# A four-layer attention kernel: the row factors of the softmax on ScalarE, a new order of value sums and casts, and the last four steps turned by TensorE

## What is computed

```python
x = _rmsnorm(hidden_states, ln_weight)             # hidden_states: layer-normed rows
h_q = (x @ w_q.T).reshape(b, lq, H, DH)            # H = 32, DH = 128
h_k = (key_value_states @ w_k.T).reshape(b, lk, H, DH)
h_v = (key_value_states @ w_v.T).reshape(b, lk, H, DH)
score = jnp.einsum('bqhd,bkhd->bhqk', h_q, h_k)
score = score + position_bias[None]
score = jnp.where(m, score, -jnp.inf)
score = jax.nn.softmax(score, axis=-1)
score = jnp.where(m, score, 0.0)
attn = jnp.einsum('bhqk,bkhd->bqhd', score, h_v).reshape(b, lq, H * DH)
out = attn @ w_out.T
return hidden_states + out
```

## Time and profile before

| | |
|---|---|
| median of three runs | 1003.94 us (1002.92 to 1004.36) |
| profiled execution | 1005.09 us, its span 1003.1 us |
| mean granted TensorE clock | 0.985 |
| busy: PE, DVE, ACT, POOL | 937.3, 739.3, 598.3, 527.0 us |

### The profile page before, as it was taken

How to read it: one execution, slowest core, us unless ns; L and a number is a source line. 1 busy time by engine, 2 the same in 40 slices (tenths; PEclk the granted TensorE clock), 3 DMA queues, 4 the chain that set the end, 5 groups by cost and what they waited for, 6 DMA issues and landing times.

```text
span 1003.1 us, 17307 instructions
## 1 busy us (share of the span) xinstructions
PE 937.3 (93%) x5261; PEld 796.9 (79%) x5261; DVE 739.3 (74%) x1289; ACT 598.3 (60%) x1847; POOL 527.0 (53%) x582
## 2 busy tenths in 40 slices
PE   9999999999899989998999899989999897889997
PEld 8778888888788878887888778877887776768885
DVE  5676874676787787777787778777877887667787
ACT  5787556465565656665666566656574656344564
POOL 2450636365557656675457555755565643112477
PEclk9999999999999999999999999999999998899999
DMA  9214348644666457645683657364755662130101
GB/s 337 78 65 151 126 153 289 215 167 147 221 223 224 148 213 253 235 146 209 215 269 123 239 184 258 123 248 155 269 166 194 204 216 84 65 116 1 33 22 63
DMA packets 61291, 171.70 MB, mean 171 GB/s; under 512 B 6055, under 2 KB 8491, under 8 KB 60988
## 3 DMA queue, kind: packets, MB, share of 16 engines
q1 hardware_dynamic: 61244, 171.11, 49.6%
HBM read 159.56 MB, written 11.53 MB: 171 GB/s over the span
## 4 chain that ended last, share of the span: by engine, by line
PE 66%; DVE 14%; ACT 8%; issue 8%; POOL 3%; DVEq 1%; DMA 0%; SPq 0%; ACTq 0%; POOLq 0%
PE ps_v L363 5%; PE ps_o L363 5%; PE ps_s L2193 5%; PE ps_o L365 4%; PE ps_o L364 4%; PE ps_v L365 4%; PE ps_v L364 4%; PE ps_q L363 4%; PE ps_q L365 4%; PE ps_q L364 4%; PE ps_k L363 4%; PE ps_k L364 4%; PE ps_k L365 4%; PE ps_t L2214 3%; ACT probs_t L799 3%
## 5 line engine op out<-in xcount | busy, mean ns | idle before, releaser
L799 ACT COPY probs_t<-scores 32x128 f32<-32x128 f32 x768 | 227.6, 296 | 175.8 <-DVE scores L1617 167.6
L787 ACT ACTIVATE scores<-scores,neg_max 128x128 f32<-128x128 f32 x256 | 99.7, 391 | 110.1 <-DVE neg_max L1602 109.7
L1158 POOL TENSOR_TENSOR wq_lo<-raw_q,wq_hi 128x256 fp32r<-128x256 f32 x65 | 57.2, 881 | 150.5 <-ACT wq_hi L620 150.5
L363 PE MATMUL ps_o<-wo_hi,att_hi 128*128 128x512 f32 x256 | 106.4, 416 | 20.0 <-DVE acc L1488 16.2
L1598 DVE TENSOR_TENSOR scores<-ps_s,shift 128x512 f32<-128x512 f32 x64 | 44.2, 691 | 104.4 <-PE ps_s L2193 104.2
L364 PE MATMUL ps_o<-wo_lo,att_hi 128*128 128x512 f32 x256 | 102.4, 400 | 0.0
L365 PE MATMUL ps_o<-wo_hi,att_lo 128*128 128x512 f32 x256 | 102.4, 400 | 0.0
L1488 DVE TENSOR_TENSOR acc<-ps_o,acc 128x512 f32<-128x512 f32 x128 | 86.8, 678 | 17.2 <-PE ps_o L365 17.1
L1476 DVE TENSOR_TENSOR att_lo<-ps_t,att_hi 128x512 fp32r<-128x512 f32 x64 | 44.2, 690 | 65.6 <-ACT att_hi L781 65.6
L1117 POOL TENSOR_TENSOR shift<-bias_sb,mask_sb 128x512 f32<-128x512 f32 x64 | 87.2, 1365 | 1.5 <-DVE scores L1598 1.5
L363 PE MATMUL ps_v<-wv_hi,ct_hi 128*128 128x256 f32 x264 | 78.0, 295 | 6.3 <-DVE vv L1442 2.2
(11 more groups left out here) (394 smaller groups left out, 2850.5 us busy)
## 6 DMA issues: line engine op xcount, KB each, us to landing
ring_hi<-scratch_x_t SPq DMA_DIRECT2D x39, 512.0 KB, 4.0
ring_lo<-scratch_x_t SPq DMA_DIRECT2D x39, 512.0 KB, 4.9
ring_hi<-scratch_c_t SPq DMA_DIRECT2D x39, 512.0 KB, 5.4
ring_lo<-scratch_c_t SPq DMA_DIRECT2D x39, 512.0 KB, 6.2
raw_o<-in_w_o SPq DMA_DIRECT2D x16, 512.0 KB, 3.3
raw_q<-in_w_q SPq DMA_DIRECT2D x15, 512.0 KB, 4.1
raw_k<-in_w_k SPq DMA_DIRECT2D x15, 512.0 KB, 5.2
xt_hi<-scratch_x_t SPq DMA_DIRECT2D x13, 512.0 KB, 5.8
```

The lines of the kernel that those rows point to most:

```text
L363: pe.matmul(dst, hi_l, hi_r, start=first, stop=False)
L787: e = act.activation(probs[n][:, m, :], scores[n][:, m, :], ACT.Exp, bias=neg_max[:, n, m:m + 1], accum_out=row_sum[:, n, m:m + 1])
L799: last = act.copy(block_of(probs_t, j, i), block_of(scores[n], i, j))
L1158: pool.tensor_tensor(w_slot(wq_lo, slot), src, w_slot(wq_hi, slot).bitcast(F32), ALU.subtract).then_inc(wq_lo_s, 1)
```

## The change

1. `scale_rows` is new: for steps 0 to 59 ScalarE multiplies the four tiles by their row factors, with four ACTIVATE Identity instructions whose scale is the column `row_fac`, right behind `attention_high`. VectorE's multiply stays in steps 60 to 63 alone. VectorE makes the row factors (`row_factors`) earlier in its step, and its two transposes wait for ScalarE's signal `scaled`.
2. On VectorE the value sums `v_c22`, `v_u4` (c=0) move ahead of the transposes, others ahead of `add_output` of part 0; in c=3 and c=7 the add of part 0, which stood ahead of the transposes, now stands behind them.
3. On ScalarE the casts of the value weights (`high_v1` to `high_v7` but 4) move ahead of the exponentials, `attention_high` directly behind these; on GpSimd the value weights' low halves come first in their step.
4. On TensorE `output` waits for `att_hi` alone and does the four matmuls that need it first; `att_lo` is waited for ahead of the last two of part 0. In c=1 a unit for k moves ahead of the one for v, in c=4 one for q.
5. In steps 60 to 63 TensorE turns the four tiles (`step_transpose`, into `ps_t`), ScalarE copies them out at once (`pt_evac`), and the values are multiplied within the same step. The order of these steps on TensorE, VectorE and ScalarE is written anew.

No DMA is added, removed or moved.

```diff
+            def scale_rows(s, n):
+                act.wait_ge(s_chain, chain(s, 3))
+                for m in range(4):
+                    e = act.activation(probs[n][:, m, :], probs[n][:, m, :], ACT.Identity, scale=row_fac[:, n, m:m + 1])
+                e.then_inc(scaled, 1)
...
+            def pt_evac(s):
+                act.wait_ge(pt_done, s - WHOLE + 1)
+                act.copy(probs_t[:], blocks(ps_t)).then_inc(pt_out, 1)
...
-            def softmax_back(s, n):
+            def row_factors(s, n):
                 dve.wait_ge(e_done, s + 1)
                 dve.reciprocal(row_inv[:, n, :], row_sum[:, n, :]).then_inc(s_chain, 1)
-                dve.wait_ge(s_chain, 5 * s + 2)
+                dve.wait_ge(s_chain, chain(s, 2))
                 dve.scalar_tensor_tensor(row_fac[:, n, :], row_max[:, n, :], -MASKED / 3.0, row_inv[:, n, :],
                                          ALU.is_gt, ALU.mult).then_inc(s_chain, 1)
-                dve.wait_ge(s_chain, 5 * s + 3)
-                dve.tensor_tensor(probs[n][:], probs[n][:], row_fac[:, n, :].unsqueeze(2).broadcast_to([P, 4, P]),
-                                  ALU.mult).then_inc(s_chain, 1)
 
             def turn_blocks(s, n):
-                dve.wait_ge(s_chain, 5 * s + 4)
+                dve.wait_ge(scaled, s + 2)
                 dve.transpose(flat(probs_t), flat(probs[n])).then_inc(s_chain, 1)
                 dve.transpose(flat(probs[n]), flat(probs[n])).then_inc(p_done, 1)
...
             def output(s, c, g=None, parts=(0, 1)):
 
-                wait_from(pe, att_lo_s, s + 1)
+                wait_from(pe, att_hi_s, s + 1)
...
                     for h in range(2):
-                        last = three(pe, ps_o[:], att_hi[:, 2 * j + h, :], att_lo[:, 2 * j + h, :],
-                                     wo_hi[:, h, :], wo_lo[:, h, :], h == 0, h == 1)
+                        pe.matmul(ps_o[:], att_hi[:, 2 * j + h, :], wo_hi[:, h, :], start=h == 0, stop=False)
+                        pe.matmul(ps_o[:], att_hi[:, 2 * j + h, :], wo_lo[:, h, :], start=False, stop=False)
+                    if j == 0:
+                        wait_from(pe, att_lo_s, s + 1)
+                    for h in range(2):
+                        last = pe.matmul(ps_o[:], att_lo[:, 2 * j + h, :], wo_hi[:, h, :], start=False, stop=h == 1)
...
+            def step_transpose(s, c):
+                pe.wait_ge(p_done, s + 1)
+                wait_from(pe, att_lo_s, s)
+                for m in range(4):
+                    last = pe.transpose(ps_t[:, m * P:(m + 1) * P], probs[c % 2][:, m, :], ident[:])
+                last.then_inc(pt_done, 1)
...
+            g = GROUPS - 1
+            s = STEPS - 4
+            wait_projections(g, 4)
+            step_scores(s, 4)
+            q_p5(g)
+            step_values(s - 1, 3, v_count(TURNS - 1, 13))
+            k_p5(g)
+            v_p4(TURNS - 1, 1)
+            output(s - 1, 3, None, (0,))
+            step_transpose(s, 4)
+            output(s - 1, 3, None, (1,))
+            step_values(s, 4, v_count(TURNS - 1, 14))
```

224 lines of the change are left out of this document (122 added, 102 removed).

## The result

The changed kernel takes 945.49 us in the median of four runs (944.07 to 946.25), the kernel before on the same chip 1003.43 (1001.01 to 1004.36): a ratio of 0.942, with an interval of 0.940 to 0.945. The forecast was 958 with a range of 944 to 984. The profiled execution took 945.47, its span 943.6.

A forecast was written before the change was run, and what follows sets the result against it. TensorE, waiting on VectorE, ScalarE or GpSimd work, was taken as the bound. Gains of 29.4 (turns), 4.5 (clock), 1.0 (small waits) and 11 (last four steps) sum to 45.9 us, giving a median of 958, range 944 to 984.

The forecast's parts named there:

- The turns: Turns 1 to 7: removing TensorE's waits gains 29.4 us, and waits of 0.3 us and less give 1.0.
- (a): Turns: ScalarE's scaling gates VectorE and waits on `acc` stay; median 973.5 us; chance 0.18 with what lies around it.
- The residue: Turns: `acc` waits left over, 0.5 us in c=3 and 0.2 in c=7 of each, 4.9 in all.
- The clock: Turns: the slow clock goes with its stall in c=0, three times at 1.5 us, 4.5 (0 to 5.4).
- The first steps: Steps ahead of turn 1: zero, as ScalarE pays 1.25 us a step and VectorE gives back 0.7 to 1.7.
- (e): Ahead of turn 1: ScalarE's extra 1.25 us in 8 steps costs 10 us unhidden, median 968; chance 0.05.
- The last four steps: Steps 60 to 63: TensorE's transposes and same-step values gain 11 us (bounds 4 and 16).
- The bursts: Last four steps: low-clock matmuls behind the waits go, three or four bursts of about 1.4 us each.
- (c): Last four steps: the clock falls behind the transposes, four bursts of 1.4 us return; median 964; chance 0.09.
- (d): Turns: late q and k low halves make TensorE wait in 56 steps; slower, median 1014 at 1 us; chance 0.05.
- The cover of 5.9 us: c=0: low halves of q and k weights end at 475.87 and are first read at 481.75, 5.9 us later.
- (b): Whole kernel: the change does all it can, 57.2 us gained, median 947; chance 0.10.

The follow-up runs named there:

- experiments 1 and 12: Kernel before with the early value-weight casts and GpSimd's subtractions alone, 1012.57 us; the same with VectorE's negation of the row maxima also gone, 992.27 us.
- experiment 8: Changed kernel with turn 1's c=3 cast, c=4's cast and subtraction, and step 0's value copy mended, and the first eight steps' multiply on VectorE: 940.68 us.
- experiment 2: Kernel before with the value sums of c=0 alone moved ahead of VectorE's multiply and transposes: 991.95 us.
- experiments 4 to 6: Changed kernel with one part undone each: last four steps as before, 960.91 us; output behind `att_lo` again, 950.33; casts and GpSimd's order as before, 968.11.
- experiment 9: Changed kernel with turn 1's c=3 cast, c=4's cast and subtraction, and step 0's value copy mended, the first eight steps' multiply staying on ScalarE: 938.27 us.
- experiment 7: Changed kernel with three more ScalarE copies that compute nothing behind the scaling in each step ahead of the last four: 959.49 us.

## Why the prediction was right in direction and 12 us short

**The turns: 29.4 and 1.0 counted, some 39 measured.** The mechanism holds. The wait for `wv_lo` in c=6 and for `vv` in c=0 are gone, and the scaling takes what was estimated. (a) fell: in turns 2 to 6 VectorE stands before its transposes for the scaling ten times, 4.8 us in all and 0.5 at most, and in c=3 not at all. The failing term is the price of a wait. The listed waits of TensorE in turns 1 to 7 fell from 37.9 to 10.7 us, by 27.2, which is less than the 30.4 of the sum; the turns became some 39 us shorter. The sum took 1.74, 1.55 and 1.2 us as the profile prints idle time, but a wait costs more than the idle time that it shows. TensorE in c=0 of turn 5 in the kernel before, at the same place as the earlier trace rows but at a full clock:

```profile
579.24 0.39 PE L365 MATMUL ps_o<-wo_hi,att_lo 128*128 128x512 f32 x1
581.36 0.39 PE L363 MATMUL ps_v<-wv_hi,ring_hi 128*128 128x256 f32 x1 [1.73 <-DVE vv L1561]
581.58 0.28 PE L364 MATMUL ps_v<-wv_lo,ring_hi 128*128 128x256 f32 x1
581.69 0.28 PE L365 MATMUL ps_v<-wv_hi,ring_lo 128*128 128x256 f32 x1
```

Matmuls overlap: those of 512 columns start every 0.23 us and those of 256 every 0.12, though one takes 0.39 or 0.28. Without the wait the matmul at 581.36 would have started at 579.47, which is 1.89 us sooner and not 1.73; and the one after it starts 0.22 behind it and not 0.12. So the wait costs 1.99, and c=0 did become 2.00 shorter. In c=6 1.55 of idle became 1.81, in this kernel and in experiments 1 and 12. Read in this way, the six listed waits of turn 5 in the kernel before have 5.7 us of idle time and cost 7.3, and the two that are left in after have 0.7 and cost 1.3. That makes 6.0 of the 6.6 us that the turn became shorter; the rest lies in delays of 0.4 us and less that the table of waits doesn't list. In c=7, where the forecast had a wait of 0.6 for `acc`, 1.42 was gained: by the starts `acc` cost 0.85, `kt` behind it 0.49, and an unlisted delay at `att_lo` 0.37, and 0.3 is left.

**The residue: 4.9 counted, 4.8 measured, but elsewhere.** The sum left `acc` 0.5 us in c=3 and 0.2 in c=7 of each turn. In turns 2 to 6 neither stands in the table of waits any more: the add of part 0 in c=3 is in time, since ScalarE had scaled before VectorE came to the transposes. What is left is 0.24 in c=1 of turns 2 to 7, 1.74 in c=3 of turn 1, and 1.63 in c=3 of turn 7, where it was 1.62. That the sums agree is luck. Besides, there are two waits that the prediction didn't see.

First, c=4 is half a microsecond longer in each turn: the negation and GpSimd's subtraction, moved to the front, meet. VectorE, GpSimd and TensorE of after:

```profile
400.92 1.09 DVE L1623 TENSOR_SCALAR neg_max<-row_max 128x4 f32<-128x4 f32 x1
401.93 0.68 DVE L1583 TENSOR_TENSOR v_odd_low<-ps_v,v_odd_low 128x512 f32<-128x512 f32 x1
...
400.70 1.29 POOL L1226 TENSOR_TENSOR wv_lo<-raw_v_even,wv_hi 128x512 fp32r<-128x512 f32 x1 [3.68 <-ACT wv_hi L682]
...
402.66 0.39 PE L372 MATMUL ps_v<-wv_hi,ct_hi 128*128 128x256 f32 x1 [0.49 <-DVE v_odd_low L1583]
```

The prediction asked for each edit what is queued behind it on its own engine. It didn't ask what a GpSimd instruction at a new time does to VectorE, although it had read that pattern itself (1.74 against 0.69 for the multiply).

Second, turn 1 gained 3.3 us and not the 6.6 of turn 5. In c=0, where turn 5 gained 2.0, turn 1 had no wait to lose; but c=3 is 0.7 longer, where in turn 5 it is 1.45 shorter. Its cast of c=3 stands ahead of the exponentials and reads a weight that is free only when the last plain value product has run. ScalarE, then TensorE:

```profile
196.67 0.62 ACT L682 CAST wv_hi<-raw_v_even 128x512 fp32r<-128x512 f32 x1 [9.34 <-PE ps_v L374]
197.20 0.40 ACT L796 ACTIVATE scores<-scores,neg_max 128x128 f32<-128x128 f32 x1
...
199.36 0.50 PE L2206 MATMUL ps_o<-wo_hi,att_hi 128*128 128x512 f32 x1 [1.40 <-ACT att_hi L790]
...
202.99 0.48 PE L2206 MATMUL ps_o<-wo_hi,att_hi 128*128 128x512 f32 x1 [1.74 <-DVE acc L1510]
```

The exponentials wait behind the cast. "For which ScalarE waits anyway" was true of the turns that the prediction had looked at and not of turn 1. In experiment 8 the first wait is gone and the second is 0.88 us, as in the kernel before.

**The clock: 4.5 counted, about 4.2 measured.** The three dips in turns 2 to 6 went; experiment 2, which moves nothing but the sums of c=0, takes them away too. A new one came in step 0, which the next paragraph prices.

**The first steps: 0 counted, -1.5 measured.** 0.9 of this lies ahead of the first scores, whose start differs by 1.1 us (32.78 to 33.90) among the runs that share after's code up to there. s=0 is 2.1 us longer: VectorE's transposes wait for the scaling, the copy of the first value part stands behind them, and TensorE waits for it, 2.05 us where it was 1.47. The granted clock of the step is 0.89 (the last row has the window, its length, and the clock as the third number from the end):

```profile
45.05 0.39 PE L372 MATMUL ps_v<-wv_hi,ct_hi 128*128 128x256 f32 x1 [2.05 <-DVE vv L1464]
...
33.90:49.52 15.62, 13.47 (x85) 12.11 (x86) 9.04 (x13) 14.25 (x36) 4.58 (x2) 0.89 0.11 36
```

In experiments 4 to 6 the same wait, 2.06 to 2.07 us, comes without that fall of the clock, and s=0 is 0.6 longer than before; so 0.6 is the wait and 1.5 the clock. The other seven steps are 1.4 us shorter. This is the edge of (e); the 10 us of that rival are not there. Experiments 8 and 9 show that taking the wait away brings most of it back a step later: in experiment 9 s=0 is 3.8 shorter than in after and s=1 2.8 longer.

**The last four steps: 11 counted (4 to 16), 17.8 measured.** The mechanism is right, and its size was beyond the upper bound. 12.7 us of waits went down to 1.4 and not to 5.5: of the four new waits that the sum counted, one of 1.1 and one of 0.2 came. Much of the rest is the clock. The stretches from the scores of s=60, 61 and 62, before:

```profile
827.51:841.81 14.30, 10.56 (x53) 8.34 (x52) 10.78 (x17) 10.32 (x35) 4.20 (x3) 0.92 0.45 144
841.81:854.65 12.84, 10.64 (x50) 8.97 (x49) 9.74 (x14) 8.12 (x25) 5.38 (x4) 0.82 0.04 9
854.65:878.53 23.88, 20.27 (x89) 16.33 (x88) 14.69 (x25) 7.44 (x26) 1.22 (x1) 0.86 0.18 66
```

and after:

```profile
785.77:797.48 11.71, 10.55 (x66) 8.96 (x64) 10.08 (x15) 6.97 (x20) 4.21 (x3) 1.00 0.60 205
797.48:806.55 9.07, 9.04 (x54) 7.68 (x53) 6.89 (x13) 5.20 (x15) 5.44 (x4) 1.00 0.17 61
806.55:824.93 18.38, 18.14 (x95) 14.60 (x93) 13.94 (x24) 5.27 (x15) 1.63 (x1) 1.00 0.22 78
```

TensorE does more matmuls after (215 for 192) in less busy time (37.7 for 41.5 us). The bursts were counted as three or four at 1.4 us; the mean clocks of the three windows say that TensorE spent some 13.6 us of them at the lower level (twice 0.08 x 14.30, 0.18 x 12.84 and 0.14 x 23.88), idle time included. How the 17.8 us split beyond the 11.3 of waits, into clock, restarts and the transposes that were added, the runs don't tell.

**(c) is not seen.** Behind the one round of transposes with a wait the next matmul takes 0.47 and then 0.39 us, the times of the full level:

```profile
794.44 0.66 PE L2244 MATMUL ps_t<-ident,scores 128*128 128x128 f32 x4 [1.12 <-DVE scores L1640]
795.13 0.47 PE L2206 MATMUL ps_o<-wo_hi,att_hi 128*128 128x512 f32 x1
795.43 0.39 PE L2207 MATMUL ps_o<-wo_lo,att_hi 128*128 128x512 f32 x1
```

The Trainium skill, "TensorE: Matmul & The Clock Gate", Part 4, says that transposes in the transpose mode don't count as busy for the clock gate. By that rule a wait of 1.12 and the transposes behind it would be one hole; no run here shows a fall of the clock from it.

**(d) is not seen as it was put.** TensorE doesn't wait for `wq_lo` or `wk_lo` in the turns, in after or with 0.99 us more on ScalarE (experiment 7). Extra time on ScalarE is felt elsewhere, and at a fifth. The cover of 5.9 us was also read too small: the matmul at 481.75 is of a product for q, whose low half GpSimd had ready at 473.35, 8.4 us sooner, and the low half for k that ends at 475.87 is not read before the next product for k, 11.5 us later:

```profile
487.33 0.40 PE L363 MATMUL ps_k<-ct_hi,wk_hi 128*128 128x512 f32 x1
```

**Where chances were misplaced.** The case that came, (b), had 0.10. The arguments against it were that the tail would have new first waits, of which most didn't come, and the prediction lacked the restart behind a wait, which adds to every wait removed. That the time fell at (b)'s 947 is in part luck: (b) had 35.8 us of waits in the turns, 5.4 for the clock and 16 in the tail, and what came was 39.1, 4.2 and 17.8, with 1.5 lost in the first steps.
